# Output projection ahead of the value product on TensorE, in stage two of a gated cross-attention and channel-mix kernel

## What is computed

```python
x = x + tanh(g_xattn[0]) * xattn(layernorm(x), ctx, ctx, mask, q_w, q_b, k_w, k_b, v_w, v_b, o_w, o_b)
x = x + tanh(g_ffn[0]) * ffn(layernorm(x), W_r, W_k, W_v, mu_r, mu_k)

# the end of xattn: the output projection
out = einsum('bsd,ed->bse', ctx, o_w) + o_b

# ffn
x_prev = concatenate([zeros((B, 1, C)), x[:, :-1, :]], axis=1)
xr = mu_r * x + (1 - mu_r) * x_prev
xk = mu_k * x + (1 - mu_k) * x_prev
r = sigmoid(einsum('btc,dc->btd', xr, W_r))
k = einsum('btc,dc->btd', xk, W_k)
out = r * einsum('btc,dc->btd', square(relu(k)), W_v)
```

## Time and profile before

| | us |
|---|---|
| median of 3 runs | 1136.81 |
| lowest, highest | 1136.52, 1137.53 |
| the profiled execution's own time | 1136.81 |
| its span, first to last instruction | 1135.0 |

### The profile page before, as it was taken

The page is one execution under the profiler, slowest core; times in us unless marked ns, Lnnn a source line. Parts: engine busy times, 40 slices in busy tenths (PEclk is TensorE's granted clock), DMA queues, the critical chain, the costliest instruction groups (busy, mean ns, idle before and its releaser), DMA issues.

```text
span 1135.0 us, 21607 instructions
## 1 busy us (share of the span) xinstructions
PE 1116.8 (98%) x7228; PEld 898.1 (79%) x7228; DVE 867.7 (76%) x1966; ACT 684.7 (60%) x1527; POOL 367.4 (32%) x595
## 2 busy tenths in 40 slices
PE   6999999999999999999999999999999999999998
PEld 5777777778778777877777877877888888888887
DVE  7878887888788887888788877887666766666765
ACT  4767776777777776777677777774233323332232
POOL 0153143045026016214404500845433344333421
PEclk9999999999999999999999999999999999999999
DMA  8585675774676577567577447923221123111201
GB/s 291 167 231 147 172 214 141 194 197 129 192 206 163 145 195 215 152 171 214 139 186 207 125 143 209 249 78 103 88 80 56 57 71 97 57 56 56 76 19 38
DMA packets 95854, 162.49 MB, mean 143 GB/s; under 512 B 13312, under 2 KB 22912, under 8 KB 95616
## 3 DMA queue, kind: packets, MB, share of 16 engines
q1 hardware_dynamic: 85760, 144.43, 45.1%
q10 hardware_dynamic: 9984, 16.68, 5.0%
HBM read 109.91 MB, written 49.57 MB: 141 GB/s over the span
## 4 chain that ended last, share of the span: by engine, by line
PE 96%; DVE 2%; DMA 1%; issue 1%; ACT 0%; SPq 0%; DVEq 0%; ACTq 0%
PE bank L588 30%; PE bank L657 19%; PE bank L619 15%; PE bank L648 10%; PE bank L669 10%; PE bank L627 8%; PE bank L799 1%; PE bank L680 1%; PE bank L788 1%; DVE neg_s L1132 0%; DMA q_stack<-qk_dram 0%; DMA x_rows<-x 0%; PE bank L612 0%; PE bank L634 0%; DVE wv_lo L1064 0%
## 5 line engine op out<-in xcount | busy, mean ns | idle before, releaser
L957 ACT ACTIVATE probs<-neg_s,negmax 128x512 f32<-128x512 f32 x512 | 368.0, 720 | 53.9 <-DVE negmax L1132 51.8
L1132 DVE CUSTOM_DVE_ANT_0 neg_s<-bank,mask_big 128x512 f32<-128x512 f32 x512 | 344.2, 680 | 10.2 <-PE bank L648 2.2
L657 PE MATMUL bank<-ident,probs 128*128 128x128 f32 x2048 | 307.9, 273 | 0.8 <-DVE pT L1138 0.8
L657 PEld LDWEIGHTS bank<-ident,probs 128*128 128x128 f32 x2048 | 248.3, 140 | 48.5 <-issue 3.1
L1138 DVE COPY pT<-bank 128x512 f32<-128x512 f32 x254 | 175.1, 689 | 110.7 <-PE bank L657 109.6
L648 PE MATMUL bank<-k_stack,q_stack 96*128 96x512 f32 x512 | 242.0, 473 | 1.4 <-DMA q_stack<-qk_dram 1.4
L964 ACT COPY pT<-bank 128x512 f32<-128x512 f32 x258 | 149.6, 580 | 130.6 <-PE bank L657 130.1
L669 PE MATMUL bank<-pT,v_sb 128*32 128x512 f32 x1024 | 116.5, 595 | 0.7
L1036 ACT ACTIVATE relu<-bank 128x512 f32<-128x512 f32 x32 | 19.1, 598 | 143.0 <-PE bank L588 143.0
L648 PEld LDWEIGHTS bank<-k_stack,q_stack 96*128 96x128 f32 x512 | 97.4, 190 | 2.8 <-DMA q_stack<-qk_dram 1.7
L1480 POOL TENSOR_TENSOR o_sb<-o_sb,w_raw 128x1024 f32<-128x1024 f32 x15 | 36.6, 2442 | 189.6 <-DVE o_sb L1354 189.6
(11 more groups left out here) (164 smaller groups left out, 2138.9 us busy)
## 6 DMA issues: line engine op xcount, KB each, us to landing
k_stack<-qk_dram SPq DMA_DIRECT2D x93, 256.0 KB, 5.4
q_stack<-qk_dram SPq DMA_DIRECT2D x93, 256.0 KB, 6.1
cT_raw<-ctxT SPq DMA_DIRECT2D x8, 1024.0 KB, 7.8
rden_bc<-rden_dram SPq DMA_DIRECT2D x128, 64.0 KB, 6.3
ctx_dram<-ctx_sb SPq DMA_DIRECT2D x32, 256.0 KB, 2.2
c_raw<-ctx_dram SPq DMA_DIRECT2D x16, 512.0 KB, 4.3
x_in<-x SPq DMA_DIRECT2D x16, 512.0 KB, 5.2
qk_dram<-k_hi SPq DMA_DIRECT2D x31, 256.0 KB, 2.9
```

What stands on the lines that cost most here:

```text
L657: mm = nc.tensor.transpose(pt_bank[i % 2][:, a * P:(a + 1) * P], probs[:, i % P_RING, a * P:(a + 1) * P], ident[:])
L957: nc.scalar.activation(probs[:, i % P_RING, :], neg_s[:, i % SM_RING, :], ACT.Exp, bias=negmax[:, k:k + 1], scale=-1.0, accum_out=den[:, g ...
L1132: nc.vector.tensor_tensor_reduce(neg_s[:, i % SM_RING, :], s_bank[tile_no(b, c, i) % S_BANKS][:], mask_big[:, q, :], 1.0, 3e38, ALU.add, A ...
```

## The change

In TensorE's `step2`, `o_proj(b + 1, h)` is issued ahead of `v_proj(b, h)`. Nothing else is edited: the other engines' programs, the waits, the banks and the buffers are the same.

```diff
                 elif not is_last(b):
                     transposes(b + 1, 0)
-                v_proj(b, h)
                 if not is_last(b):
                     o_proj(b + 1, h)
+                v_proj(b, h)
 
             for b in range(B):
                 step2(b, 0)
```

## The result

The changed kernel takes 1185.6 us (median of 3 runs, 1184.72 to 1187.59) against 1136.81: the ratio is 1.0439, with a 95% interval of 1.0421 to 1.0456. The forecast was 1177 with a range of 1161 to 1185. The direction and the loop through y were right, but the time lies 0.6 us above the range: TensorE's clock fell in eight steps, which the sum had at nothing.

What follows compares the result with a forecast made beforehand. TensorE was taken as the bound, busy for the whole steady step. Step 0's 0.7, 13 x 2.9 = 37.7 and step 14's 2.1 sum to 40.5 us: span 1135.0 to 1175.5, time 1177, range 1161 to 1185.

Steps and rivals of the forecast that it cites:

- the loop through y: Late V delays y, GpSimd's add, the next residual, root and xh, then T and O: 2.9 us a step.
- c_lo alone costs nothing in a steady step, and 0.7 in step 0: O behind T waits for c_lo: 0.4 us to spare in steady steps, 0.7 us lost in step 0.
- Residual at 3.63, behind the add: VectorE's residual waits for GpSimd's add of the late y: starts 3.63 behind K, 4.19 us late.
- rival (b): Residual does not hang on the late y's add; only step 0's 0.7 is left: 1137.5 us, chance 0.06.
- One root operation held under kact_lo: On GpSimd, VectorE's kact_lo now overlaps the inverse root and holds one operation, costing 1.1 or 0.8 us, taken as 0.95.
- Rival (a): The loop is late but kact_lo does not hold the root: 1.95 us a step, 1164 us, chance 0.14.
- xh at 12.6, O at 14.8, step of 26.06: Times behind K: xh starts at 12.6, O at 14.8 instead of 11.99, next K at 26.06; 2.9 us a step.
- O's getting under way: On TensorE, O's first matmul group behind a wait starts up more slowly: 0.1 us a step.
- Step 14 at 2.1: Step 14 has no O, but T waits for xh, to 13.3 against 11.20: 2.1 us.
- rival (c): The chain costs more: further GpSimd operations held (1191 us) or TensorE's granted clock falling (5.8 us a step, 1252); chance 0.08.
- the quarter of a step at half speed: If a quarter of TensorE's 23.16 us step ran at 1.2 GHz: 5.8 us more a step, 1252.
- Its sign for the clock: A fallen TensorE clock would show as PEclk below 9 in the profile page's slices of stage two.

Runs made afterwards that it cites:

- both legs cut: Changed kernel with four halves of x1, GpSimd's root ahead of the add and bias, and kact_lo behind c_lo: 1136.3 us, ratio 1.0003.
- every-second kernel: Changed kernel with V ahead of O again in the even steps, so only odd steps have the change: 1150.5 us, ratio 1.0128.
- the two filled kernels: Changed kernel with extra matmuls in TensorE's waits: eight between R and T, 1174.6 us; or three between T and O, 1173.1 us.
- the first cut of the loop: Changed kernel with four halves of x1 instead of two, so the residual waits for an add two units older: 1169.8 us, ratio 1.03.

## Where the prediction was right, and which term failed

- **What bounds the kernel, and that the new order can gain nothing**: right. With both legs cut, the new order gives the old time, 1.0003.
- **c_lo alone costs nothing in a steady step, and 0.7 in step 0**: right. Odd steps of the every-second kernel take 23.15; step 0 of the changed kernel grew by 0.74.
- **y held by V's late end, to 0.26**: right, 0.20. **Residual at 3.63, behind the add**: right, 3.58, so rival (b) falls.
- **One root operation held under kact_lo, at 9.99 or 10.27, for 1.1 or 0.8 us**: it was the one at 9.85, for 1.25 instead of 0.19, so 1.06. Shown by taking it away: O 1.04 earlier. Rival (a) falls.
- **xh at 12.6, O at 14.8, step of 26.06**: 12.51, 14.70 and 25.88. The forecast's 2.9 a step was 2.7: the 0.1 for O's getting under way was counted twice, since V's start behind T in the old step carried the same (its first group lasted 1.18, and O's behind the wait in an ordinary step lasts 1.20), and O came 0.1 earlier than forecast. That makes the sum 2.3 us too high.
- **Step 14 at 2.1**: 2.0. **Fourteen steps pay**: right, shown by the every-second kernel. **It doesn't grow**: right.
- **The clock** is the term that failed. The prediction named it in rival (c), which had a chance of 0.08, nearly all of it for further held operations, and left it out of the sum and out of the range. It cost 1.5 us in each of eight steps, 12.2 us in all. The step that failed is in the sentence that the new waits would be "about 2 us before T and under 1 us before O, each step": the waits came out as forecast, and the clock's term for them stayed at nothing because "No row here shows it". The rows of before could not show it, since their steady steps have no wait on TensorE.
- The Trainium skill, "TensorE: Matmul & The Clock Gate", section "A second HAM failure mode: psum-queue depth-cycling", which the prediction cited, says that the clock can swing between its two levels when TensorE idles a little and often between groups of matmuls. The trace of after agrees as far as the fall goes: with idles of 1.64 and 0.43 us in a step the granted clock went to 0.50 in eight steps of thirteen. The idles here are waits for xh and c_lo.
- **The prediction's sizes for the clock**: the quarter of a step at half speed (5.8 us) was too much. It is a stretch of about 3 us, which costs half of itself. Its sign for the clock, a slice of the page below 9, could not show this either, as every slice still reads 9.
- **Without the clock** the changed kernel takes 1173 to 1175 us (the two filled kernels), against the forecast of 1177. From the forecast span of 1175.5 to the measured 1183.8 are 8.3 us: 12.2 more from the clock, 2.3 less from the thirteen steps, 0.1 less from step 14 and 1.5 less from stage one and the tail. That the time came within 1 us of the range is luck: the errors partly cancel.
- **The range** ended at 1185 and the time is 1185.6. It left out case (c) on purpose, although the new waits were of the kind that case (c) named, and that was the wrong case to leave out.

Beyond the prediction, my expectation for the first cut of the loop was wrong by 14 us: I moved VectorE's work earlier and did not ask under which GpSimd instruction it would then stand.

## What to carry to other kernels

Before moving a product behind another on the busiest engine, ask who waits for its end and how far back the loop closes. Here V's end released y, and y's buffer released the next unit's layer norm. The slack was worth half of the move and not the whole. When a change puts waits on TensorE, price the clock too: look at the waits of a step together and not one by one, and read the granted clock in slices of 1 us, since a mean over a step or a page's slice hides it.

## What the runs showed of the hardware

- **TensorE's clock fell after waits that are short one by one.** 2.0 us ahead of eight transposes and 0.7 us behind them, after 11 us of matmuls with hardly a wait, took the granted clock from 1.00 to 0.50 for about 3 us, in eight steps of thirteen. Either of the two alone did so in none. Filling 0.7 us with three useless matmuls made the kernel 12 us faster.
- **VectorE and GpSimd hold each other for whole instructions, in both directions.** GpSimd's 0.19 became 1.25 under a VectorE subtraction of two SBUF operands; VectorE's subtraction of 1.19 became 3.35 under a GpSimd add. The Trainium skill, "SBUF — State Buffer", section "Who interferes with whom", says this of VectorE instructions with two SBUF inputs beside GpSimd ones that read SBUF. These runs agree.
- **VectorE's xh, which has one tensor input, was held too.** This was seen once: in the kernel before with kact_lo late, step 0, xh stands across GpSimd's bias and the two instructions take 3.10 us instead of 0.99:

```profile
780.40 3.10 DVE L1297 TENSOR_SCALAR xh<-w_raw,mv,rstd 128x512 f32<-128x512 f32 x2
...
780.77 2.45 POOL L1461 TENSOR_TENSOR x_in<-x_in,tgbo 128x1024 f32<-128x1024 f32 x1 [0.86 <-DMA x_in<-x]
```
